# Masked hexagonal convolution with group norm: eight slots loaded at first, loads six chunks ahead instead of seven

## The chip, the cores and the metric

The kernel runs on one core of one Trainium2 chip. The metric is device time in microseconds (us). Before the change it is 741.6 us, the median of three runs (741.59 to 742.24). The engines are named as in the profile: PE is the matrix engine, PEld its weight loads, DVE the vector engine, ACT the scalar engine, POOL GpSimd, and SP the engine that here only issues DMAs. A DMA's bytes are moved by 16 DMA engines; "issuing" is what SP does, "landing" is when all 16 have written their part and the semaphore shows it.

## The reference

`x` is 2048 images x 64 channels x 16 x 16 pixels, float32 (134.2 MB). The output has the same shape.

```python
def reference(x, w_up, b_up, w_left, b_left, w_right, b_right):
    xn = _gn(x)                       # group norm, 32 groups: 2 channels x 256 pixels share mean and variance
    xp = pad(xn, 1 on each side)
    xp[:, :, DST_R, DST_C] = xp[:, :, SRC_R, SRC_C]      # 30 border pixels are copied around
    up    = conv(xp, w_up    * _UP,    stride 2) + b_up     # five of the 4x4 taps are used in each
    left  = conv(xp, w_left  * _LEFT,  stride 2) + b_left
    right = conv(xp, w_right * _RIGHT, stride 2) + b_right
    out = zeros; out[0::2, 0::2] = up; out[1::2, 0::2] = left; out[1::2, 1::2] = right
    return x + out * OUT_MASK
```

All of `x` has to be read once and all of the output written once: 268.4 MB in all.

## The kernel before

The 2048 images are 64 chunks (`NCHUNK`) of 32. Of each pair of images one lies in partitions 0 to 63 and one in 64 to 127 (64 channels each), so a chunk is a tile of 128 partitions x 16 x 256 elements, 2 MB (2.097 million bytes). It lies in one of eight slots (`SLOTS`) of the tile `xs`; chunk k uses slot k % 8. The result is added in place, so a slot holds a chunk from its load until its store has landed. Loads and stores are made in two halves of 1 MB each, half 0 and half 1 (pairs 0 to 7 and 8 to 15). Each half of a load has a semaphore of its own per slot (`loaded`); the two halves of a store share one per slot (`stored`, 32 counts for one chunk).

All large DMAs are issued by SP, on one queue, in an order written out by hand (lines 195 to 214): three weight loads, chunk 0 in four quarters, chunks 1 to 6 in halves (line 201), and then for each chunk k, for each half: wait until chunk k is added (`bank_added`, counted by POOL), store the half (line 193 issues it), wait for `stored` of the slot that is to be loaded, load a half of chunk k + 7 (line 189 issues it). A wait stands on SP ahead of all that SP issues later.

What a chunk m goes through:

- DVE, line 229: eight `bn_stats` over the chunk, put between the small steps of the chunk before it (`moments` and `norms`, lines 233 to 273). The first four need half 0 of chunk m, the last four half 1, and `norms` of chunk m - 1 ends behind them.
- DVE (line 277) and ACT (line 313) write the normalised pairs to one of two tiles `tn`, then POOL copies the border pixels (`wrap`, line 411).
- PE: 240 matmuls into four banks of PSUM (line 459), of which a second set of four exists.
- ACT copies the banks with their bias to `res` (`evacuate`, line 336). In its order this stands two chunks later (`LAG`), ahead of the normalising of chunk m + 2.
- POOL adds `res` into `xs` (`add`, line 401, 12 instructions for a chunk, in four banks with one count of `bank_added` each), likewise ahead of `wrap` of chunk m + 2. For the last chunk SP stores half 0 once its adds are done.

Of the kernel before, what the change touches and what calls it, by code (L numbers as in the profile page):

```python
# [17 lines left out]
NCHUNK = B // (2 * G)  # L18
SLOTS = 8
# [43 lines left out]

QUARTER = G // 4
HALF = (slice(0, G // 2), slice(G // 2, G))
AHEAD = 7


WRAPS = [
# [22 lines left out]
def hex_conv(nc, x, w_up, b_up, w_left, b_left, w_right, b_right, out):  # L92
    ctx = ExitStack()
    with ctx:
# [3 lines left out]
        def sem(name):  # L98
            return ctx.enter_context(nc.semaphore(name))
# [26 lines left out]
        def w_raw(t):  # L126
            at = C * 16 * W_AT[t][1]
            return tn[1][W_AT[t][0]:W_AT[t][0] + C, at:at + C * 16]
# [6 lines left out]
        stored = [sem(f"stored{s}") for s in range(SLOTS)]  # L135
# [46 lines left out]
        @block.sync  # L182
        def _(sp):
            def part(dram, k, pairs):
                return dram[k][:, pairs], xs[:, k % SLOTS, :].rearrange("p (g q) -> p g q", g=G)[:, pairs]

            def load(k, half):
                frm, to = part(x_dram, k, HALF[half])
                sp.dma_start(to, frm).then_inc(loaded[half][k % SLOTS], 16)

            def store(k, half):
                to, frm = part(out_dram, k, HALF[half])
                sp.dma_start(to, frm).then_inc(stored[k % SLOTS], 16)  # L193

            for t, w in enumerate((w_up, w_left, w_right)):
                sp.dma_start(w_raw(t), w.rearrange("o c a b -> o (c a b)")).then_inc(w_loaded[t], 16)
            for n in range(4):
                frm, to = part(x_dram, 0, slice(QUARTER * n, QUARTER * (n + 1)))
                sp.dma_start(to, frm).then_inc((quarter[n // 2], loaded[n // 2][0])[n % 2], 16)
            for k in range(1, AHEAD):  # L200
                for half in range(2):
                    load(k, half)

            for k in range(NCHUNK):
                n = k + AHEAD
                for half in range(2):
                    sp.wait_ge(bank_added, NB * (k + 1) if k < NCHUNK - 1 else NB * k + 4 + 2 * half)
                    store(k, half)
                    if n < NCHUNK:
                        if n >= SLOTS:  # L210
                            sp.wait_ge(stored[n % SLOTS], 32 * (n // SLOTS))
                        load(n, half)
            for s in range(SLOTS):
                sp.wait_ge(stored[s], 32 * (NCHUNK // SLOTS))
# [155 lines left out]
        def _(pool):  # L370
# [34 lines left out]
            def wrap(k):  # L405

                b = k % 2
                pool.wait_ge(t_dve, k + 1)
                pool.wait_ge(t_act, k + 1)
                for dst, src, dims in WRAPS:  # L410
                    last = nc.gpsimd.tensor_copy(view(tn[b], dst, [(T_PAIR, G)] + [(d, n) for d, _, n in dims]),  # L411
                                                 view(tn[b], src, [(T_PAIR, G)] + [(d, n) for _, d, n in dims]))
                last.then_inc(t_ready, 1)
# [98 lines left out]
```

## Time and profile before

| | us |
|---|---|
| median of 3 runs | 741.6 |
| profiled execution, its time | 742.11 |
| its span | 740.3 |
| DVE busy | 613.8 (83%) |
| PE busy | 655.8 (89%) |
| ACT busy | 574.8 (78%) |
| POOL busy | 473.9 (64%) |
| moved by DMA | 269.62 MB, mean 364 GB/s |

The span is from the first to the last instruction of the execution; the 1.8 us between it and the time lie outside it. DMA issues have durations of their own on SP, which are not counted as busy. A matmul's end is modelled, so PE's share is rather high.

### The profile page before, as it was taken

How to read it: one execution, taken by the hardware profiler on the slowest of the kernel's cores; microseconds unless marked ns; L12 is line 12 of the kernel's file. 1: busy time of each engine (PE TensorE's matmuls, PEld its weight loads, DVE VectorE, ACT ScalarE, POOL GpSimd, SP SyncE). 2: the span in 40 equal slices, each digit the busy share in tenths (PEclk: the TensorE clock that was granted, in tenths of full speed). 3: DMA queues.
4: the chain of work that ended last, by engine and by line, in shares of the span. 5: the costliest groups of instructions: out<-in, count | busy, mean ns of one | idle time of the engine just before them, and what ended most of it. 6: DMA issues, size and time to landing. Idle time of an engine off the chain costs nothing.

```text
span 740.3 us, 36046 instructions
## 1 busy us (share of the span) xinstructions
PE 655.8 (89%) x15484; PEld 602.8 (81%) x15484; DVE 613.8 (83%) x1793; ACT 574.8 (78%) x1235; POOL 473.9 (64%) x1109
## 2 busy tenths in 40 slices
PE   1699999999999989889889898898898988989893
PEld 1589999999999888778788787787887878878883
DVE  4999999999999778788787787887977878878740
ACT  3488888988888787787877877878778778787782
POOL 1177777787776765756657657566576575665774
PEclk9989999999999999999999999999999999999997
DMA  8999999999999999999999999999999999999998
GB/s 262 349 362 384 384 380 373 367 367 374 374 356 366 366 367 370 365 379 368 366 369 367 374 370 367 374 365 362 379 361 375 362 366 376 365 365 374 378 352 286
DMA packets 267034, 269.62 MB, mean 364 GB/s; under 512 B 4656, under 2 KB 266800, under 8 KB 266992
## 3 DMA queue, kind: packets, MB, share of 16 engines
q1 hardware_dynamic: 266512, 269.24, 106.0%
q14 instruction: 38, 0.31, 0.1%
q10 hardware_dynamic: 480, 0.00, 0.0%
q8 instruction: 4, 0.07, 0.0%
HBM read 135.01 MB, written 134.22 MB: 364 GB/s over the span
## 4 chain that ended last, share of the span: by engine, by line
DMA 36%; DVE 31%; ACT 12%; POOL 10%; SPq 4%; issue 3%; PE 3%; POOLq 0%; ACTq 0%
DMA xs<-in_x 35%; DVE stats L229 17%; ACT tn L313 12%; DVE tn L277 7%; POOL xs L401 5%; POOL tn L411 4%; SPq L193 3%; PE bank L459 3%; DVE small L261 2%; DMA out<-xs 1%; DVE nmr L272 1%; DVE small L265 1%; DVE rstd L268 1%; DVE var L250 1%; DVE mate L237 0%
## 5 line engine op out<-in xcount | busy, mean ns | idle before, releaser
L459 PE MATMUL bank<-tn,wts 64*64 64x192 f32 (+1 forms) x15360 | 646.9, 325 | 0.0
L459 PEld LDWEIGHTS bank<-tn,wts 64*64 64x64 f32 x15360 | 593.4, 137 | 34.1
L229 DVE BATCH_NORM_STATS2 stats<-xs 128x6 f32<-128x512 f32 x512 | 350.4, 697 | 95.1 <-DMA xs<-in_x 95.1
L401 POOL TENSOR_TENSOR xs<-res,xs 128x192 f32<-128x192 f32 (+6 forms) x775 | 376.1, 530 | 7.7 <-ACT res L336 5.8
L313 ACT ACTIVATE tn<-xs,nmr,rstd 128x256 f32<-128x256 f32 x511 | 258.9, 592 | 78.7 <-DVE nmr L272 78.1
L336 ACT ACTIVATE res<-bank,bias 64x512 f32<-64x512 f32 (+5 forms) x640 | 302.1, 472 | 21.1 <-PE bank L459 10.9
L411 POOL COPY tn<-tn 128x128 f32<-128x128 f32 (+2 forms) x320 | 97.3, 362 | 242.2 <-ACT tn L313 242.2
L277 DVE TENSOR_SCALAR tn<-xs,rstd,nmr 128x256 f32<-128x256 f32 x513 | 181.5, 427 | 2.3
L470 PEld LDWEIGHTS bank<-blank 128*128 128x128 f16 x64 | 6.1, 96 | 82.5 <-ACT res L336 65.8
L470 PE MATMUL bank<-blank 128*128 128x2 f16 x64 | 11.2, 176 | 63.9 <-POOL tn L411 63.8
L307 ACT ACTIVATE std<-var 128x16 f32<-128x16 f32 x64 | 13.8, 216 | 49.7 <-DVE var L250 49.7
L261 DVE SCALAR_TENSOR_TENSOR small<-var,small 128x16 f32<-128x16 f32 x64 | 26.4, 412 | 0.1
L265 DVE TENSOR_TENSOR small<-small 128x16 f32<-128x16 f32 x64 | 19.6, 306 | 0.1
L250 DVE SCALAR_TENSOR_TENSOR var<-gap,m 128x16 f32<-128x16 f32 x64 | 19.5, 304 | 0.1
L268 DVE SCALAR_TENSOR_TENSOR rstd<-small 128x16 f32<-128x16 f32 x64 | 18.1, 283 | 0.1
L258 DVE RECIPROCAL small<-std 128x16 f32<-128x16 f32 x64 | 14.8, 232 | 1.0 <-ACT std L307 1.0
L272 DVE SCALAR_TENSOR_TENSOR nmr<-msum,rstd 128x16 f32<-128x16 f32 x64 | 13.7, 214 | 0.1
L237 DVE STREAM_SHUFFLE mate<-stats 128x48 f32<-128x48 f32 x64 | 13.0, 204 | 0.0
L439 PE MATMUL bank<-ident,tn 64*64 64x64 f32 x60 | 3.5, 316 | 8.6 <-ACT tn L177 8.6
L242 DVE TENSOR_TENSOR m<-stats,mate 128x16 f32<-128x16 f32 x64 | 11.1, 173 | 0.0
L243 DVE TENSOR_TENSOR msum<-stats,mate 128x16 f32<-128x16 f32 x64 | 11.0, 172 | 0.0
L245 DVE SCALAR_TENSOR_TENSOR gap<-gap 128x16 f32<-128x16 f32 x64 | 10.7, 167 | 0.0
(18 smaller groups left out, 24.1 us busy)
## 6 DMA issues: line engine op xcount, KB each, us to landing
out<-xs SPq DMA_DIRECT2D x128, 1024.0 KB, 11.1
xs<-in_x SPq DMA_DIRECT2D x126, 1024.0 KB, 11.1
xs<-in_x SPq DMA_DIRECT2D x4, 512.0 KB, 8.4
tn<-in_L_conv_w_up SPq DMA_DIRECT2D x1, 256.0 KB, 3.8
tn<-in_L_conv_w_left SPq DMA_DIRECT2D x1, 256.0 KB, 4.3
tn<-in_L_conv_w_right SPq DMA_DIRECT2D x1, 256.0 KB, 6.2
bias<-in_L_conv_b_up ACTq DMA_DIRECT2D x2, 0.2 KB, 4.5
bias<-in_L_conv_b_left ACTq DMA_DIRECT2D x2, 0.2 KB, 6.0
```

What stands on the lines that cost most here:

```text
L193: sp.dma_start(to, frm).then_inc(stored[k % SLOTS], 16)
L229: last = nc.vector.bn_stats(stats[:, k % 2, 2 * u:2 * u + 2].rearrange("p g a -> p (g a)"), both)
L250: nc.vector.scalar_tensor_tensor(var[:], gap2[:], EPS * GROUP, m2[:], op0=ALU.add, op1=ALU.add).then_inc(var_ready, 1)
L261: nc.vector.scalar_tensor_tensor(small[:, 1], var[:], -0.5 / GROUP, small[:, 0], op0=ALU.mult, op1=ALU.mult).then_inc(stat_step, 1)
L265: nc.vector.tensor_tensor(small[:, 2], small[:, 1], small[:, 0], ALU.mult).then_inc(stat_step, 1)
L268: nc.vector.scalar_tensor_tensor(rstd[:], small[:, 2], 1.5, small[:, 0], op0=ALU.add, op1=ALU.mult).then_inc(stat_step, 1)
L277: last = nc.vector.tensor_scalar(t_image(b, g), x_image(s, g), rstd[:, g:g + 1], nmr[:, g:g + 1], ALU.mult, ALU.add)
L313: last = nc.scalar.activation(t_image(k % 2, g), x_image(k % SLOTS, g), ACT.Identity, bias=nmr[:, g:g + 1], scale=rstd[:, g:g + 1])
L336: last = nc.scalar.activation(res[onto, BANK_AT[j] + at:BANK_AT[j] + at + cols], psum[NB * b + j][banks, at:at + cols], ACT.Identity, bias ...
L401: last = nc.gpsimd.tensor_tensor(onto, frm, onto, ALU.add)
L411: last = nc.gpsimd.tensor_copy(view(tn[b], dst, [(T_PAIR, G)] + [(d, n) for d, _, n in dims]), view(tn[b], src, [(T_PAIR, G)] + [(d, n) fo ...
L459: last = nc.tensor.matmul(psum[bank + j][to:to + C, at:at + cols], wts[first:first + C, NT * rect[0] + n, :], taps(b, rect, tap, first), s ...
```

## The change

`AHEAD` is 6 instead of 7. The loads before the loop run over chunks 1 to 7 instead of 1 to 6, so that all eight slots are filled. In the loop, loads of chunks below 8 are left out (they are loaded already), and every other load of chunk n = k + 6 waits for the store of the slot's last chunk, n - 8 = k - 2, where before it was chunk k - 1. The first load of the loop is then chunk 8 at k = 2; before it was chunk 7 at k = 0. The last load, chunk 63, is issued at k = 57 instead of k = 56. Nothing but SP's order is changed.

```diff
-AHEAD = 7
+AHEAD = 6
...
-            for k in range(1, AHEAD):
+            for k in range(1, SLOTS):
                 for half in range(2):
                     load(k, half)
...
                 for half in range(2):
                     sp.wait_ge(bank_added, NB * (k + 1) if k < NCHUNK - 1 else NB * k + 4 + 2 * half)
                     store(k, half)
-                    if n < NCHUNK:
-                        if n >= SLOTS:
-                            sp.wait_ge(stored[n % SLOTS], 32 * (n // SLOTS))
+                    if SLOTS <= n < NCHUNK:
+                        sp.wait_ge(stored[n % SLOTS], 32 * (n // SLOTS))
                         load(n, half)
```

## Rows read from the trace of the kernel before

**Rows 1.** The page: DMA's busy tenths and GB/s in 40 equal slices

```profile
DMA  8999999999999999999999999999999999999998
GB/s 262 349 362 384 384 380 373 367 367 374 374 356 366 366 367 370 365 379 368 366 369 367 374 370 367 374 365 362 379 361 375 362 366 376 365 365 374 378 352 286
```

**Rows 2.** Waits from 200 to 700 us: who waited for whom, us, times, longest

```profile
SPq L189 <- DMA out<-xs: 131.5, 43, 3.3
...
DVE stats L229 <- DMA xs<-in_x: 84.9, 43, 2.4
```

**Rows 3.** SP's timeline, one steady iteration and its neighbours: start us, duration us, instruction

```profile
297.66 0.37 SPq L189 DMA_DIRECT2D xs<-in_x  x1
298.07 2.43 SPq L193 DMA_DIRECT2D out<-xs  x1
300.55 2.76 SPq L189 DMA_DIRECT2D xs<-in_x  x1
303.35 2.63 SPq L193 DMA_DIRECT2D out<-xs  x1
309.02 0.37 SPq L189 DMA_DIRECT2D xs<-in_x  x1
...
684.80 0.37 SPq L189 DMA_DIRECT2D xs<-in_x  x1
```

**Rows 4.** DMA issues by line: count, KB, median us from issue to landing

```profile
out<-xs SPq DMA_DIRECT2D x128, 1024.0 KB, 11.1
xs<-in_x SPq DMA_DIRECT2D x126, 1024.0 KB, 11.1
```

**Rows 5.** One iteration in stretches: PE, PEld, DVE, ACT, POOL busy, PEclk, DMA share, GB/s

```profile
303.40:306.40 3.00, 3.00 (x99) 3.00 (x93) 2.96 (x13) 2.75 (x6) 0.48 (x2) 1.00 1.09 383
306.40:309.00 2.60, 2.03 (x64) 1.71 (x56) 2.60 (x10) 2.00 (x5) 1.17 (x4) 1.00 1.09 378
309.00:312.00 3.00, 2.52 (x41) 2.13 (x45) 0.92 (x3) 2.89 (x7) 3.00 (x7) 1.00 1.03 334
312.00:315.00 3.00, 3.00 (x68) 2.86 (x64) 3.00 (x8) 1.25 (x4) 3.00 (x8) 1.00 1.04 350
```

**Rows 6.** From 0 to 411.7 us, by line: adds (12 a chunk) and stores (2 a chunk)

```profile
L401 POOL TENSOR_TENSOR xs<-res,xs x420: 332/506/852, 37.2 to 405.7; 128x288 f32<-128x288 f32 x35, 128x192 f32<-128x192 f32 x35, 128x96 f32<-128x96 f32 x35, 128x64 f32<-128x64 f32 x35
L193 SPq DMA_DIRECT2D out<-xs x65: 1563/2542/3530, 43.1 to 405.5; - x65
```

**Rows 7.** Stretches of 20 us, columns as in rows 5

```profile
20.00:40.00 20.00, 13.97 (x270) 12.32 (x274) 19.92 (x56) 9.15 (x20) 5.75 (x15) 0.91 1.10 349
...
80.00:100.00 20.00, 20.00 (x484) 18.56 (x482) 19.93 (x57) 17.42 (x38) 14.51 (x34) 1.00 1.09 383
...
700.00:720.00 20.00, 18.98 (x466) 17.57 (x462) 11.79 (x34) 17.06 (x37) 14.74 (x35) 1.00 1.05 358
```

**Rows 8.** SP's timeline, start and early iterations

```profile
6.15 35.67 SPq L189 DMA_DIRECT2D xs<-in_x  x12
43.15 1.56 SPq L193 DMA_DIRECT2D out<-xs  x1
...
69.94 0.37 SPq L189 DMA_DIRECT2D xs<-in_x  x1
...
115.10 0.37 SPq L189 DMA_DIRECT2D xs<-in_x  x1
```

**Rows 9.** POOL's timeline: the adds of chunks 1 (two rows) and 2

```profile
47.37 4.57 POOL L401 TENSOR_TENSOR xs<-res,xs 128x288 f32<-128x288 f32 x8
52.72 1.79 POOL L401 TENSOR_TENSOR xs<-res,xs 128x112 f32<-128x112 f32 x4 [0.78 <-ACT res L336]
...
58.35 6.09 POOL L401 TENSOR_TENSOR xs<-res,xs 128x288 f32<-128x288 f32 x12
```

**Rows 10.** The chain of waits that ended last: the last load and what follows it

```profile
687.70 11.15 DMA xs<-in_x
...
698.87 0.72 DVE stats L229
...
708.21 9.98 PE bank L459 x184
...
718.29 10.05 PE bank L459 x193
...
731.54 2.54 POOL xs L401 x10
```

**Rows 11.** SP's timeline and its last wait

```profile
690.48 44.00 SPq L193 DMA_DIRECT2D out<-xs  x14
...
SPq L214 <- DMA out<-xs: 5.1, 1, 5.1
```

## The prediction

> **What bounds the kernel now.** I read the page's slices first. The DMA engines are busy in tenths of 9 from the second slice to the last but one, at 356 to 384 GB/s [rows 1], while no compute engine is full. The waits come next: from 200 us on DVE waits for loads 43 times, once a chunk, 84.9 us in all, and SP waits as often for stores, 131.5 us in all, about 3.1 us each [rows 2]. So the kernel is bound by DMA, and there is one visible hole in the issuing of it. The question is whether that hole costs anything.
>
> SP's timeline shows an iteration k: load of k+7 half 0 at 297.66, store of k half 1 at 298.07, load half 1 at 300.55, store of k+1 half 0 at 303.35 (ended 305.98), then nothing until 309.02 [rows 3]. That is the wait for both halves of the store of k; its second half was issued at 298.07, and 11.1 us later [rows 4] is 309.2. The iteration is 309.02 - 297.66 = 11.36 us; over the 33 iterations from 309.02 to 684.80 the mean is 375.78 / 33 = 11.39 us [rows 3]. It moves four halves, 4.194 MB, so 368 GB/s.
>
> A DMA that finds room takes SP 0.37 us; the others take 2.4 to 2.8 us, close to a quarter of the iteration (2.84 us) [rows 3]. I read these as SP standing at a full queue. When the wait ends at 309.02, two halves issued earlier are still under way: the load of 300.55, due at 311.7, and the store of 303.35, due at 314.5 [rows 3, 4]. A lone DMA needs little to get going: after the last store is issued SP waits 5.1 us, of which 2.7 us is the data at full rate, so about 2.7 us is latency [rows 11]. 5.4 us of work stand in the queue and 2.7 us are needed: on the path that sets the landings the queue never runs empty.
>
> Yet there is a dip. During the wait the engines move 378 to 383 GB/s, after it 334 and 350 for six us [rows 5]. A share of 1.03 instead of 1.09 says that some of the 16 engines are idle. The early rows tell which: at 80 to 100 us the engines move 383 GB/s [rows 7], but SP gets only 4.194 MB through in (115.10 - 69.94) / 4 = 11.29 us, 371 GB/s [rows 8]. More is moved than completed, so most engines run ahead of at least one that is slower, and landing means the slowest. I conclude that the dip is the idling of engines that are ahead, and that the slowest one, which is never out of work, sets 11.3 to 11.4 us with or without the wait.
>
> **The change part by part.**
>
> *The wait.* It now asks for the store of k - 2, issued about 20 us before with 11.1 us to land: it never blocks. SP will stand at the full queue instead; its instructions grow from 2.4 to 2.8 us and the 0.37 us ones too. The value of this is the uncertain term, over 56 iterations (loads of chunks 8 to 63). Best case: all engines at 383 GB/s [rows 5, 7], 10.95 us an iteration, 0.44 less, so -24.6 us. Nearer row: the iterations before the wait had much to do, 11.29 [rows 8], -0.10 each, -5.6 us. On the other side the engines that no longer idle compete with the slowest; the trace has no row for it, and I allow the same 0.10, +5.6 us (the far end would be the 349 GB/s of loads alone [rows 7], 12.0 us). I take 0, since the queue of the slowest engine is unchanged.
>
> The Trainium skill (Perfetto Trace Analysis, What "DMA-bound" means) would read long DMA instructions on the issuing engine as descriptor generation, a bound of its own. The 0.37 us rows speak against it here. If it held, SP would be freed by the change and only the bandwidth limit would be left, which is the first rival below. The skill's page DMA: Bandwidth & Descriptors (Specifications) gives 368 GB/s as the vendor's derated figure, which the steady part hits; by it nothing could be gained. The 383 GB/s row exceeds it, so I don't lean on it.
>
> *Cover for stores.* At 411.7 us POOL has done 420 adds, 35 chunks, and SP has issued 65 stores, the last (chunk 32, half 0) at 405.5, when the adds of chunk 34 end [rows 6]. So a chunk lies finished for two iterations, 22.8 us, before SP stores it. With loads one chunk less ahead this becomes one iteration, 11.4 us. It still covers: no wait for POOL appears in the steady part.
>
> *The order at the end.* This is the step on the path. Since chunks wait for their load and DMA is always behind, the end is set by the landing of chunk 63's half 1. Before it in the queue stand all loads and, now, the stores of chunks 0 to 56; after the change of 0 to 57. One chunk of store more, 2.097 MB, half an iteration: 11.39 / 2 = +5.7 us (5.5 at 383 GB/s, 6.0 at 349). After that landing comes a chain of compute that no DMA is part of: statistics at 698.87, normalising, the convolutions of chunks 62 (708.21) and 63 (718.29), adds until 734.08, and the last store [rows 10], then 5.1 us of waiting [rows 11]. From 698.87 to the end at 740.3 is 41.4 us and stays. Before, seven chunks of store (41 us of DMA) were hidden under it, now six; the DMA queue is simply empty sooner. So the store taken out of the tail saves nothing, and put ahead of the last load it costs all.
>
> *The start.* SP issues the first 12 halves in 35.67 us, 2.97 each, to 41.8 [rows 8]. Now chunk 7 follows until 47.8, chunk 0's store until 53.7 (its adds were ready at 43.15), chunk 1's from 54.5 on, when its adds end, and then SP has nothing until the adds of chunk 2 end at 64.4 [rows 9]. Is the queue empty by then? Landings run at 2.9 to 3.0 us: the last first-phase load issued at 38.8 lands about 50.5, the two of chunk 7 by 56.4, four store halves by 68. At 64.4 there is 3.6 us of work, more than the 2.7 of latency. So no gap, at most 1.5 us if the stores run faster. The reordering itself costs a little: two loads at 2.97 instead of 2.84, and four store halves without loads beside them, at 358 GB/s (the nearest row, mostly stores [rows 7]) 2.93 instead of 2.84: 0.3 + 0.4 = +0.6 us. Filling the eighth slot earlier gains nothing, as the compute is not short of loads in the first 100 us and the order behind it decides.
>
> *Sum* for the profiled execution: 742.11 + 0 + 5.7 + 0.6 = 748.4 us. The median of the runs is 0.5 below the profiled one, so I predict 747.9.
>
> **The rivals.**
>
> *Freed queue.* The wait starves all engines alike, the dip is the loss, and without it an iteration is 10.95 us: 747.9 - 24.6 = 723. For it: the dip sits exactly behind the wait [rows 5]. Against it: 5.4 us of work in the queue at that moment, and an early stage at 383 GB/s in which an iteration still took 11.29. This rival decides from 0.11 us an iteration on (6.3 / 56), where it pays for the later last load. 9 in 100; anything between 723 and 738.
>
> *Part of it.* The iteration returns to the 11.29 of the early stage or a little below: -5.6, or up to -9. 742.3, within the noise or slightly faster. 17 in 100.
>
> *Crowding.* Engines that never idle slow the slowest by 0.10 us an iteration: 753.5 us. 8 in 100.
>
> *Stores wait for POOL.* If a chunk's way from landing to its adds grows by over 11.4 us, the cover is gone and the loop is closed through POOL; nothing in the rows does that. 2 in 100, 755 or more.
>
> *That the change does nothing* would need the end not to follow the last load; the chain says that it does [rows 10].
>
> **How the numbers follow.** The forecast has 64 in 100, with 744.5 to 751 as its own range. The range goes from 738 to 753: it takes in most of the second rival and the lower part of crowding, and leaves out the freed queue. A change of 0.2% (1.5 us) is about what can be told from none. Faster by more: 9 from the freed queue, 8 from the second: 0.17. Within: 9 from it, 1 from the forecast's edge: 0.10. Slower: 0.73.
>
> **What would show it.** SP's timeline: no gap of 3 us ahead of a load, all four issues near 2.8 us, an iteration of 11.3 to 11.5. The GB/s of the steady part still near 368. The last load issued about 6 us later than 687.70 and landing near 705, and 41.4 us from there to the end. In the start a gap on SP from about 57 to 64.4. I am wrong if the iteration is below 11.27 (then something other than one slow engine was the limit), if the tail behind the last load is shorter than 41 us, or if SP waits for POOL after 100 us.

## The result and the profile after

The changed kernel takes 747.48 us (median of 4 runs, 747.14 to 747.81), the kernel before 741.6: a ratio of 1.0082, 95% interval 1.0069 to 1.0096. It is slower by 5.9 us; 747.9 was predicted. Its profiled execution took 747.14 us with a span of 745.3, 5.0 above that of before (742.11 and 740.3).

The page after, its GB/s in 40 slices, and the waits of DVE for loads and of SP over the whole span (who waited for whom: us, times, longest):

```profile
GB/s 264 349 352 365 383 385 384 383 376 370 365 365 372 368 374 367 368 370 367 375 368 368 367 367 375 372 368 367 369 369 369 366 368 370 367 371 370 374 294 225
...
DVE stats L228 <- DMA xs<-in_x: 104.3, 50, 9.4
...
SPq L193 <- POOL xs L400: 171.0, 114, 8.6
SPq L213 <- DMA out<-xs: 5.1, 1, 5.1
```

The wait for stores, 131.5 us from 200 to 700 us [rows 2], is gone from the list. The steady GB/s is what it was [rows 1]. The largest difference is in the last two slices: 294 and 225 where before 352 and 286 stood. Smaller ones are at the start: 365 instead of 384 in the fourth slice, and 384 and 383 instead of 373 and 367 in the seventh and eighth. (The view lists a wait of SP's stores for POOL. In the kernel before it is listed too, 88.3 us in 86 pieces from 200 to 700 us. In the steady part of both kernels it is put on issues that follow one another without a gap, of chunks whose adds had ended about an iteration earlier or more, so there it is the full queue and not POOL.)

SP's timeline of the kernel after, an iteration, a later one, and the end (start us, duration us):

```profile
300.05 2.96 SPq L189 DMA_DIRECT2D xs<-in_x  x1
303.06 2.62 SPq L193 DMA_DIRECT2D out<-xs  x1
305.72 2.77 SPq L189 DMA_DIRECT2D xs<-in_x  x1
308.53 2.62 SPq L193 DMA_DIRECT2D out<-xs  x1
311.20 3.03 SPq L189 DMA_DIRECT2D xs<-in_x  x1
...
419.42 2.79 SPq L189 DMA_DIRECT2D xs<-in_x  x1
...
686.80 2.98 SPq L189 DMA_DIRECT2D xs<-in_x  x1
689.83 2.65 SPq L193 DMA_DIRECT2D out<-xs  x1
692.52 2.75 SPq L189 DMA_DIRECT2D xs<-in_x  x1
695.31 44.21 SPq L193 DMA_DIRECT2D out<-xs  x12
```

This is the picture that was forecast: no gap, and issues of 2.6 to 3.0 us, four in each iteration. An iteration is (686.80 - 300.05) / 34 = 11.375 us; before it was 11.387 [rows 3]. So 3.1 us of waiting were taken out of every iteration, and the iteration is only 0.01 us shorter. SP now spends at the full queue the time that it had spent at the semaphore.

The chain after, from the last load on (start us, duration us):

```profile
692.52 11.19 DMA xs<-in_x
...
703.73 0.71 DVE stats L228
...
713.25 9.97 PE bank L458 x189
...
723.33 10.05 PE bank L458 x193
...
736.58 2.54 POOL xs L400 x10
```

Set beside [rows 10]: the last load is used at 703.73 instead of 698.87, 4.9 us later, and from there to the end of the span it is 41.6 us instead of 41.4. Between these two executions nearly the whole difference is the time of this one landing. Behind it the DMA engines now have so little left to move that they idle, which is the 294 and 225 GB/s.

### The profile page after: what moved, and what is told of

It reads as the page before. It is cut to its first block, busy times and chain, and to the rows that moved or that the text cites. A ratio compares the mean times of both kernels' runs of the same rounds, so it can differ in the third digit from the quotient of the medians.

```text
span 745.3 us, 36046 instructions
## 1 busy us (share of the span) xinstructions
PE 656.6 (88%) x15484; PEld 603.8 (81%) x15484; DVE 609.6 (82%) x1793; ACT 575.0 (77%) x1235; POOL 471.6 (63%) x1109
## 4 chain that ended last, share of the span: by engine, by line
DMA 37%; DVE 28%; ACT 13%; POOL 10%; SPq 4%; issue 3%; PE 3%; POOLq 0%; ACTq 0%
DMA xs<-in_x 37%; DVE stats L228 15%; ACT tn L312 13%; DVE tn L276 5%; POOL xs L400 5%; POOL tn L410 5%; SPq L193 4%; PE bank L458 3%; DVE small L260 2%; DVE small L264 1%; DVE rstd L267 1%; DVE nmr L271 1%; DVE mate L236 0%; SPq L189 0%; DVE var L249 0%
## 5 line engine op out<-in xcount | busy, mean ns | idle before, releaser
L276 DVE TENSOR_SCALAR tn<-xs,rstd,nmr 128x256 f32<-128x256 f32 x513 | 178.6, 421 | 2.3
L271 DVE SCALAR_TENSOR_TENSOR nmr<-msum,rstd 128x16 f32<-128x16 f32 x64 | 12.2, 191 | 0.1
## 6 DMA issues: line engine op xcount, KB each, us to landing
out<-xs SPq DMA_DIRECT2D x128, 1024.0 KB, 11.3
```

Of the source, the lines that this page charges most:

```text
L271: nc.vector.scalar_tensor_tensor(nmr[:], msum[:], -0.5, rstd[:], op0=ALU.mult, op1=ALU.mult).then_inc(norm_ready, 1)
L276: last = nc.vector.tensor_scalar(t_image(b, g), x_image(s, g), rstd[:, g:g + 1], nmr[:, g:g + 1], ALU.mult, ALU.add)
```

## The experiments

Each kernel was run beside the kernel before on the same chip. The kernels with one engine beside the copy have two runs each, the others four to eleven.

| kernel | ratio to before (95% interval) | median us, before beside it |
|---|---|---|
| eight slots first, seven ahead | 1.0042 (1.0028 to 1.0055) | 744.22, 741.25 |
| before with half semaphores | 1.0004 (0.9995 to 1.0013) | 741.29, 741.25 |
| changed, seven ahead from chunk 50 | 1.0015 (1.0006 to 1.0024) | 741.98, 741.25 |
| five ahead | 1.0227 (1.0213 to 1.0241) | 757.85, 741.25 |
| six ahead alone | 1.0113 (1.0097 to 1.0128) | 749.57, 741.21 |
| half semaphores, load first | 0.9998 (0.9989 to 1.0007) | 740.97, 741.21 |
| copy, seven ahead | 0.9610 (0.9595 to 0.9625) | 712.52, 741.21 |
| copy, eight first and six ahead | 0.9615 (0.9601 to 0.9630) | 712.96, 741.21 |
| copy and PE | 0.9852 (0.9823 to 0.9880) | 730.07, 741.05 |
| copy and DVE | 0.9687 (0.9659 to 0.9715) | 717.89, 741.05 |
| copy and POOL | 0.9651 (0.9623 to 0.9679) | 715.21, 741.05 |
| copy and ACT | 0.9659 (0.9631 to 0.9687) | 715.81, 740.95 |

### The wait by itself

```diff
-    stored = [sem(f"stored{s}") for s in range(SLOTS)]
+    stored = [[sem(f"stored{s}_{half}") for s in range(SLOTS)] for half in range(2)]
...
-    sp.wait_ge(stored[n % SLOTS], 32 * (n // SLOTS))
+    sp.wait_ge(stored[half][n % SLOTS], 16 * (n // SLOTS))
```

> The kernel before, seven ahead, its order of DMAs untouched, but each half of a store has its own semaphore, so a load of a half waits only for the store of the same half, 8 to 11 us older than the one it waited for. SP's wait should shrink from 3.1 us to near nothing. Theory (the wait costs nothing, the landings of the slowest DMA engine set the pace): 741.6 us within 1 us, an iteration of 11.3 to 11.4 us, the dip in GB/s still there. Rival (the wait is worth 0.10 us an iteration and the changed kernel gained it but paid for it elsewhere): 736. Rival (freed queue): 717 to 725.

It took 1.0004 of the time before. SP's timeline in it, and four stretches (columns as in rows 5):

```profile
294.31 2.93 SPq L189 DMA_DIRECT2D xs<-in_x  x1
297.28 3.02 SPq L193 DMA_DIRECT2D out<-xs  x1
300.34 2.77 SPq L189 DMA_DIRECT2D xs<-in_x  x1
303.16 2.65 SPq L193 DMA_DIRECT2D out<-xs  x1
305.86 2.98 SPq L189 DMA_DIRECT2D xs<-in_x  x1
```

```profile
303.00:306.00 3.00, 3.00 (x97) 3.00 (x92) 2.96 (x10) 2.59 (x6) 0.62 (x2) 1.00 1.00 338
306.00:309.00 3.00, 2.20 (x70) 1.87 (x62) 3.00 (x12) 2.38 (x6) 1.41 (x5) 1.00 1.05 365
309.00:312.00 3.00, 2.78 (x47) 2.35 (x51) 0.88 (x3) 2.91 (x6) 3.00 (x6) 1.00 1.08 369
312.00:315.00 3.00, 3.00 (x71) 2.93 (x66) 2.96 (x9) 1.11 (x5) 2.81 (x8) 1.00 1.08 376
```

The wait is gone, the order is the same, and the time is too: the wait costs nothing, to within the interval, -0.4 to +1.0 us. This falsifies the freed queue and the rival "part of it", and crowding too, since SP doesn't pause in the steady part here either. The dip, 338 GB/s, stands there without a wait in front of it. It isn't tied to one phase of the compute either: in this dip DVE is busy for 2.96 of 3.00 us and POOL for 0.62, in that of the kernel before DVE for 0.92 and POOL for 3.00 [rows 5].

### The end of the order by itself

```diff
+TURN = 50
...
+                ahead = (AHEAD,) if k < TURN else (AHEAD, AHEAD + 1) if k == TURN else (AHEAD + 1,)
...
+                    for n in (k + m for m in ahead):
```

> The changed kernel up to chunk 49; at chunk 50 both chunk 56 and chunk 57 are loaded, and from there on loads run seven ahead, so the last load is issued at chunk 56 as before. Theory: the 5.7 us of the one chunk of stores ahead of the last load are gone, only the start's share is left: 741.5 to 742.5 us, and the last load lands near 699. Rival (the start or the steady part costs the 5.9 us): 746 to 748.

741.98 us, 0.7 above the kernel before: of the 5.9 us, 5.2 come back by moving one pair of loads ahead of the stores at chunk 50, some 75 us before the last load is issued. The last load issued on SP and the first use of its data on DVE:

```profile
686.70 2.83 SPq L190 DMA_DIRECT2D xs<-in_x  x1
689.58 44.69 SPq L194 DMA_DIRECT2D out<-xs  x14
```

```profile
697.80 0.72 DVE L230 BATCH_NORM_STATS2 stats<-xs 128x6 f32<-128x512 f32 x1 [0.77 <-DMA xs<-in_x]
```

697.80 is 5.9 us earlier than in the changed kernel and 1.1 us earlier than in the kernel before, and the span ends at 740.1. This kernel has the changed one's start and most of its steady part, so neither of them is where most of the time went. In its chain of waits the last load doesn't appear; PE's work on the last two chunks does:

```profile
708.02 9.97 PE bank L460 x176
...
718.09 10.05 PE bank L460 x191
```

With two chunks loaded close together PE had fallen behind the loads, and from 647 us on it took one chunk after the other at 10.1 us each. Its last two start within 0.2 us of when they did before [rows 10]. So the 1.1 us by which the landing is ahead brings nothing, and from the first use to the end it is 42.3 us here.

### More of the same: five ahead

Against the changed kernel:

```diff
-AHEAD = 6
+AHEAD = 5
```

> The changed kernel with five ahead instead of six: two chunks of stores more ahead of the last load than in the kernel before. Theory: another 5.7 us for the end and about 0.5 for the start, 753.5 us; a chunk now has no spare iteration between its adds and its store, so SP may wait for POOL and add 0 to 3 us: 753 to 757. Rival (the price of the change lay in something that happens once, such as the start's gap): 748 to 750.

757.85 us, 16.6 above before, and 0.9 over the upper end of my range. The span ends at 755.8; the last load is used at 714.46, and 755.8 - 714.46 = 41.3 us again. SP at the start, and the first use of the last load on DVE:

```profile
48.12 25.81 SPq L193 DMA_DIRECT2D out<-xs  x7
73.97 0.58 SPq L189 DMA_DIRECT2D xs<-in_x  x1
...
714.46 0.71 DVE L228 BATCH_NORM_STATS2 stats<-xs 128x6 f32<-128x512 f32 x1 [1.88 <-DMA xs<-in_x]
```

The landing is 15.6 us later than before: two chunks of stores are 11.4, and the other 4.2 are lost at the start. There three chunks are now stored as their adds finish, with no load between them, and the queue runs thin: the page's fourth and fifth slices have 323 and 349 GB/s, where before both had 384. I had allowed about 0.5 for the start.

### The two halves of the change

Eight slots first and seven ahead is the changed kernel with one line back:

```diff
-AHEAD = 6
+AHEAD = 7
```

> All eight slots loaded at first as in the changed kernel, but seven chunks ahead in the loop as before, so the only move against the kernel before is chunk 7's load past chunk 0's store; SP waits for stores again. Theory (what stands ahead of the last load sets the end): the same bytes stand ahead of it as before, so 742.0 us, at most 0.6 above the kernel before. Rival (the price lies in the start, in the two stores without loads and the thin queue behind them): most of the 5.9 us stays, 745 to 747.

744.22 us: 3.0 above before, which is neither what the theory nor what the rival said. The order at the end is that of before, so this is the start. SP's timeline of it:

```profile
48.07 9.01 SPq L193 DMA_DIRECT2D out<-xs  x3
62.27 0.38 SPq L189 DMA_DIRECT2D xs<-in_x  x1
62.69 0.58 SPq L193 DMA_DIRECT2D out<-xs  x1
```

Chunk 0's store now stands behind chunk 7's load, and chunk 8's load waits for it to land with only one half (chunk 1's first store) queued behind it: SP issues nothing from 57.08 to 62.27, and the issues of 0.38 and 0.58 us after that show that the queue had room for both. The page's fourth slice has 348 GB/s, where before it had 384. In the steady part the wait has two halves queued behind the awaited store, and is free; here, with one, it is not.

Six ahead alone is the kernel before with `AHEAD = 6`, so that only chunks 1 to 5 are loaded at first.

> Six ahead in the loop, but only chunks 1 to 5 loaded at first, so chunk 6's load stands behind chunk 0's store, and chunk 7's behind chunk 1's: the other half of the change by itself. Theory (the one chunk of stores more ahead of the last load costs 5.2 to 5.7 us and how the start is filled is nearly a wash): 746.5 to 748 us, as the changed kernel within 1 us. Rival (filling all slots at first is what costs, as the 3 us of the kernel with eight slots and seven ahead could suggest): 742 to 744.

749.57 us, 8.4 above before and 2.5 over the changed kernel's distance from it: 1.6 us above my range, and again the start. SP's timeline of it:

```profile
42.92 0.39 SPq L193 DMA_DIRECT2D out<-xs  x1
43.35 0.58 SPq L189 DMA_DIRECT2D xs<-in_x  x1
43.98 1.47 SPq L193 DMA_DIRECT2D out<-xs  x1
45.49 2.83 SPq L189 DMA_DIRECT2D xs<-in_x  x1
53.14 0.38 SPq L193 DMA_DIRECT2D out<-xs  x1
```

With ten halves instead of twelve to issue, SP is done with them at 35.8 and has nothing to issue until chunk 0 is added at 42.9. So loading all eight slots at first does pay, 2.5 us, once loads run six ahead: it fills what this order would leave empty. It doesn't make up for the end of the order.

### Can the end be moved the other way?

Against the kernel with half semaphores:

```diff
                 for half in range(2):
-                    sp.wait_ge(bank_added, ...)
-                    store(k, half)
                     if n < NCHUNK:
                         if n >= SLOTS:
                             sp.wait_ge(stored[half][n % SLOTS], 16 * (n // SLOTS))
                         load(n, half)
+                    sp.wait_ge(bank_added, ...)
+                    store(k, half)
```

> Seven ahead, half semaphores, and in the loop the load of a half stands before the store of the same half instead of behind it: each load, the last one too, has half a chunk of stores (1 MB, 2.8 us) less ahead of it than before. Theory of the order alone (the end is 41.4 us behind the last load): 738.5 us. Theory with both limits (in the kernel before the stores behind the last load, 14 halves at 2.9 us, end together with that chain, so the last load landing earlier leaves the stores as the limit): 740.5 to 741.5 us, no gain that can be told, with the last load landing near 696.

740.97 us, 0.9998 of before: no gain, as the theory of two limits had it. The last load was issued at 686.29 and took 8.42 us, so it landed at 694.7, 4.1 us earlier than before, and the last adds ended earlier as well:

```profile
686.29 8.42 DMA xs<-in_x
...
694.73 0.71 DVE stats L230
...
727.55 2.54 POOL xs L402 x10
```

The adds end at 730.1 instead of 734.1, but the span ends at 738.7, 44 us behind the landing: now the stores are last. So in the kernel before, the chain of compute and the stores behind the last load end nearly together. Moving that load later costs its full distance, and moving it earlier brings nothing. SP waits for stores 112 times here, 332.0 us in all, and that costs nothing either. None of the kernels that compute the whole output beats the one before.

### What sets 11.4 us an iteration

The copy kernels leave out the programs of all engines but SP, which waits for the load of a half instead of for its adds; the output is then `x`:

```diff
-                    sp.wait_ge(bank_added, ...)
+                    sp.wait_ge(loaded[half][k % SLOTS], 16 * (k // SLOTS + 1))
...
-        @block.vector  (and scalar, gpsimd, tensor)
```

> All compute is left out: SP alone, with the order of DMAs of the kernel before (seven ahead, both waits of a slot), stores what it loaded, so the output is x. It shows what the DMA engines need by themselves. Theory (the DMA engines set 11.3 to 11.4 us an iteration whatever the compute does): 64 chunks at 11.35 and about 10 us of latency at both ends, 733 to 739 us, with dips in GB/s as before. Rival (compute's traffic in the memories slows single DMA engines, and this is the dip): an iteration of 10.9 us, 384 GB/s throughout, 705 to 710 us.

> The same with the changed kernel's order (all eight slots loaded at first, six ahead), compute left out. Without the chain of compute behind the last load its place in the order is worth nothing. Theory: as the copy with seven ahead within 1 us. Rival (the order or the start costs DMA time by itself): 4 to 6 us more than the copy with seven ahead.

712.52 and 712.96 us. Between the two orders there is no difference that can be told, as theory said: without the compute behind the last load its place is worth nothing. But the pace is the rival's, 10.9 us an iteration, though the 712.5 us lie 2.5 above its range. The copy with seven ahead, its GB/s, its wait for stores, and two issues one iteration apart:

```profile
GB/s 279 348 354 385 386 386 386 386 386 386 385 384 386 386 386 386 386 386 386 386 386 385 386 386 386 386 386 386 386 386 386 386 386 386 386 386 386 386 364 300
...
SPq L189 <- DMA out<-xs: 148.0, 56, 2.8
...
308.50 0.37 SPq L189 DMA_DIRECT2D xs<-in_x  x1
...
319.38 0.37 SPq L189 DMA_DIRECT2D xs<-in_x  x1
```

10.88 us an iteration, 384 to 386 GB/s from the fourth slice to the last but two, and no dip, though SP still waits for stores, 2.6 us in each iteration. The copy with the changed order doesn't wait, and both take 10.87 us an iteration on the mean from 280 to 540 us. So the DMA engines by themselves are not held to 368 GB/s by a slow one among them; something in the compute does that. Four kernels add one engine's work to the copy with seven ahead, on tiles that no large DMA of the loop touches, in the form of this (for DVE):

```diff
+            for k in range(NCHUNK):
+                if k:
+                    dve.wait_ge(t_dve, k)
+                for u in range(G // 2):
+                    nc.vector.bn_stats(stats[...], view(tn[0], 2 * u * PIX, [(1, PIX), (PIX, 2)]))
+                for g in range(11):
+                    last = nc.vector.tensor_scalar(view(tn[1], ...), view(tn[0], ...), 0.5, 0.5, ALU.mult, ALU.add)
+                last.then_inc(t_dve, 1)
```

> The copy with seven ahead, and beside it PE alone runs the 15360 convolution matmuls of the kernel on a tile of zeros in SBUF, waiting for nothing. No other compute; the output is x. It asks which engine's traffic takes the copy's 10.9 us an iteration to the kernel's 11.4. If PE's reads of SBUF do it: 11.2 to 11.4 us an iteration, 735 us or more. If not: 712 to 715 us, 386 GB/s throughout.

> The copy with seven ahead, and beside it DVE alone runs, 64 times over, eight bn_stats and eleven normalisings like the kernel's on tiles that no large DMA touches. If DVE's traffic slows the DMA engines: over 11.1 us an iteration, 725 us or more. If not: 712 to 715 us. I think DVE or POOL more likely than PE, since they write SBUF.

> The copy with seven ahead, and beside it POOL alone runs the kernel's 12 adds and 5 border copies, 64 times over, on tiles that no large DMA touches. If POOL's traffic slows the DMA engines: over 11.1 us an iteration, 725 us or more, since in the kernel the stretches with the lowest GB/s have POOL busy throughout. If not: 712 to 715 us, and then it is several engines together or that they work on the slots being moved.

> The copy with seven ahead, and beside it ACT alone runs, 64 times over, eight normalisings like the kernel's and ten plain activations of 240 columns, from SBUF to SBUF. Beside PE alone the copy took 17.6 us more, beside DVE 5.4, beside POOL 2.7, 25.6 in all; the kernel takes about 28.6 more than the copy. If the traffic of the engines simply adds up, ACT's share is 2 to 5 us: 714.5 to 717.5. If it is more than a sum, ACT alone costs nothing: 712.5.

Over the copy's 712.5 us, PE costs 17.6, DVE 5.4, POOL 2.7 and ACT 3.3, and the four shares add up to 29.0. The kernel before stands 28.7 above its copy. The results beside PE, DVE and POOL lie between the two forecasts that I gave for each; only that beside ACT is where a forecast had it. PE's busy tenths and GB/s of the copy beside PE:

```profile
PE   5899999999999999999999999999999999500000
...
GB/s 286 350 360 382 385 385 382 375 371 377 373 363 376 371 374 367 376 381 365 375 378 374 374 375 372 377 372 374 376 371 373 365 377 374 371 386 386 386 357 300
```

From the eighth slice to the last full one of PE's work the rate is 363 to 381, and in the slice after it stops it is 386. In the fourth to the seventh it is still 382 to 385, though PE is as busy. My guess of DVE or POOL, written ahead of the run, was wrong: PE has the largest share. That the sum comes so close to the kernel's own slowdown is partly luck. The work put back is not all of the kernel's (DVE is busy for 455.2 us there and 613.8 in the kernel, ACT for 506.0 and 574.8, PE for 619.6 and 655.8), it runs without the kernel's waits, and no run has two engines beside the copy. What the runs show is that the work of each engine slows the DMAs, PE's most. By what path it does so is open.

## Why the prediction was right

**The order at the end** (+5.7 us): right in place and nearly in size. Moving one pair of loads gives 5.2 us back. The tail from the first use of the last load, 41.4 us before, measured 41.3 to 41.6 in the changed kernel and four of the others. Seven ahead from chunk 50 has 42.3, because PE was behind, and load first has 44, because the stores end last. The same order without the compute (the copies) costs nothing.

**The wait** (0): right, shown by the half semaphores (1.0004) and by both copies. The argument from the queue, 5.4 us of work against 2.7 us of latency, held, though the 5.1 us of waiting less 2.7 of data leave 2.4 and not 2.7. The kernel with eight slots first and seven ahead shows the other side of it: only one half stood behind the awaited store, and the stall did cost.

**The reason for the dip**: wrong. I concluded that engines that ran ahead were idle, and that the slowest one sets 11.3 to 11.4 us "with or without the wait". The step that failed reads 383 GB/s at 80 to 100 us against 371 issued as one engine being slower by nature. The copy has the same engines at 10.88 us, and the changed kernel itself contradicts the step, with all its compute running. Two loads of it, four iterations apart:

```profile
75.15 2.63 SPq L189 DMA_DIRECT2D xs<-in_x  x1
...
118.90 2.57 SPq L189 DMA_DIRECT2D xs<-in_x  x1
```

That is 43.75 / 4 = 10.94 us an iteration, in a stretch in which PE is busy for 19.96 of 20 us (80 to 100 us) and the engines move 384 GB/s. What takes 0.5 us an iteration later on is compute running beside the DMAs. The value of the wait came out right because this, like a slow engine, doesn't depend on how SP's time is spent; so the zero rests on the argument from the queue, and its second ground was luck. The rival "freed queue" had the right pace in mind, 10.95 us, and the wrong thing to free.

**The start** (+0.6 us): neither confirmed nor refuted; it is smaller than what one trace of each kernel can tell. By the profiled executions the sign is the other one. The second half of chunk 39's load shows it. In the kernel before it is the third of these:

```profile
411.30 0.37 SPq L189 DMA_DIRECT2D xs<-in_x  x1
411.71 2.45 SPq L193 DMA_DIRECT2D out<-xs  x1
414.20 2.76 SPq L189 DMA_DIRECT2D xs<-in_x  x1
```

In the changed kernel it is issued at 419.42, 5.2 us later; the chunk of stores ahead of it accounts for 5.7, so the start would have given 0.5 back. The stretch at 383 to 385 GB/s lasts until the eighth slice after, and until the fifth before (384 in both slices), with 380 in the sixth. From chunk 39 to the last load another 0.4 came back (4.8 in the end). But the profiled execution of the kernel before is 0.5 us above its median and that of the changed one 0.3 below, together more than that. By the medians 5.9 - 5.7 = +0.2 is left for the start, and the kernel with seven ahead from chunk 50, which has this start, is 0.7 us above before (interval 0.4 to 1.8), where PE being behind has a part too. The gap on SP that I forecast from 57 to 64.4 ran from 60.0 to 63.4. The variants of the start show how loosely I had it: by the medians, less 5.7 us for each chunk of stores at the end, +3.0 us with eight slots and seven ahead, +2.7 with six ahead alone and +5.2 with five (+4.2 by its trace). In each of them the queue runs thin while the compute has too little finished to store, and SP shows it as issues of under 0.6 us.

**Cover for stores**: right. At six ahead SP never paused in the steady part, and the wait for POOL that the view lists is the queue, as said above; at five ahead small pauses appear ahead of the first store of an iteration, with the iteration still 11.4 us.

The sum was 6.3 us; the profiled executions differ by 5.0 and the medians by 5.9. That the forecast is off by only 0.4 us is in part luck, since the terms for the wait and for the start were not as sure as that.

## What to carry to other kernels

In this kernel, which is bound by DMA, a wait of 3.1 us on the issuing engine cost nothing with two halves queued behind the awaited transfer, and did cost with one. So look at how much was issued behind that transfer, not at how long the wait is. What does count is the order: ask what must still happen after the last load lands, and how many bytes stand ahead of that load. Where the chain of compute and the remaining stores end together, as here, the load is in the right place, and a chunk of stores put in front of it costs its transfer time, 5.2 to 5.7 us.

## What the runs showed of the hardware

Compute slows DMA without touching the same tiles: 386 GB/s for the copy, 363 to 381 beside PE's matmuls on a tile of their own, and about 368 in the full kernel. What is odd is when this sets in. In the full kernels, and beside PE alone, mixed loads and stores still run at 380 to 385 GB/s until 90 to 150 us from the start of the span, although the compute is already going. Beside PE alone it is 384 GB/s from 60 to 120 us and 374 from 300 to 600, with PE busy the whole time in both. Beside DVE, POOL or ACT alone the rate first dips later still, after 179 us. So how busy an engine is doesn't settle the rate by itself, and nothing tried here explains when the slower one sets in. Loads alone move 348 to 349 GB/s, with or without compute, and loads and stores mixed 386 without compute.
